# A gather put ahead of two loads, a shorter sort and a first product in parts, at the start of a fused expert kernel

## What is computed

```python
def xattn(h, token_ids, ctx):              # 4 experts, chosen by token id
    e = min(clip(token_ids, 0, 24999) // 6250, 3)
    return (silu(h @ ctx[e].T) * (h @ ctx[e].T)) @ ctx[e].T

def ffn(h, router_w, wg, wu, wd):          # 8 experts, chosen by argmax of the router
    e = argmax(h @ router_w.T)
    g, u = bitlinear(h, wg[e]), bitlinear(h, wu[e])
    return bitlinear(square(relu(g)) * u, wd[e])

x = x + xattn(layernorm(x), token_ids, ctx)
x = x + ffn(layernorm(x), router_w, wg, wu, wd)
```

## Time and profile before

| | us |
|---|---|
| three runs | 279.82, 280.27, 280.93; median 280.27 |
| the profiled execution | 279.12 |
| its span, first to last instruction | 277.3 |
| TensorE busy | 243.5 (88%) |
| VectorE busy | 221.8 (80%) |
| ScalarE busy | 213.1 (77%) |
| GpSimd busy | 154.9 (56%) |

### The profile page before, as it was taken

The page is one execution under the profiler, slowest core; times in us unless marked ns, Lnnn a source line. Parts: engine busy times, 40 slices in busy tenths (PEclk is TensorE's granted clock), DMA queues, the critical chain, the costliest instruction groups (busy, mean ns, idle before and its releaser), DMA issues.

```text
span 277.3 us, 5763 instructions
## 1 busy us (share of the span) xinstructions
PE 243.5 (88%) x1419; PEld 175.5 (63%) x1419; DVE 221.8 (80%) x664; ACT 213.1 (77%) x322; POOL 154.9 (56%) x277
## 2 busy tenths in 40 slices
PE   2287779999999999999999999886699999999980
PEld 2134558888888888888888888762344555545440
DVE  5958797889877887778878877898968888888871
ACT  2778778798887998879889788855468888888860
POOL 3435013576565655656656553487547487576743
PEclk9997999999999999999999999999779999999996
DMA  5999259356646664956656534440486994201110
GB/s 214 430 372 345 60 195 384 109 214 224 219 156 227 208 194 154 329 183 232 227 190 219 162 131 175 146 128 8 107 294 191 306 278 173 78 34 66 57 41 0
DMA packets 13839, 51.72 MB, mean 186 GB/s; under 512 B 2862, under 2 KB 2862, under 8 KB 10224
## 3 DMA queue, kind: packets, MB, share of 16 engines
q1 hardware_dynamic: 8928, 37.91, 39.9%
q0 software_dynamic: 4880, 13.44, 13.8%
HBM read 40.49 MB, written 13.48 MB: 195 GB/s over the span
## 4 chain that ended last, share of the span: by engine, by line
PE 74%; DVE 12%; issue 6%; ACT 3%; POOL 2%; DMA 1%; DVEq 0%; POOLq 0%
PE bank L1294 36%; PE bank L1397 19%; PE bank L1287 9%; PE bank L1369 5%; PE bank L1391 4%; PE bank L1313 1%; POOL x L412 1%; DVE ctx_lo L791 1%; POOL out_rows L505 1%; DVE fac L1113 1%; DVE ternary L759 1%; DVE prod L1103 1%; ACT relu L632 1%; ACT ternary L542 1%; DMA token_ids<-token_ids_in 1%
## 5 line engine op out<-in xcount | busy, mean ns | idle before, releaser
L1397 PE MATMUL bank<-ternary,qT 128*128 x184 | 45.0, 388 | 0.4 <-ACT qT L620 0.3
L542 ACT ACTIVATE ternary<-staged 128x2048 bf16<-128x2048 f32 x22 | 42.0, 1910 | 1.3 <-DMA staged<-weight_chunks 1.2
L548 ACT ACTIVATE ternary<-staged,w_scale 128x1536 int16<-128x1536 f32 x22 | 34.4, 1566 | 2.8 <-DVE w_scale L803 2.8
L1397 PEld LDWEIGHTS bank<-ternary,qT 128*128 128x128 bf16 x184 | 18.2, 100 | 22.3 <-issue 4.7
L451 POOL DMA_INDIRECT x_rows<-row,store_at x19 | 22.2, 1168 | 16.7 <-POOL store_at L447 14.4
L412 POOL DMA_INDIRECT x<-x_rows,gather x19 | 21.1, 1108 | 18.7 <-DVE row L897 14.8
L1397 PE MATMUL bank<-ternary,rT 128*128 x92 | 24.6, 392 | 2.6 <-DVE late_rows L1132 1.2
L505 POOL DMA_INDIRECT out_rows<-late_rows x18 | 19.1, 1060 | 13.3 <-DVE late_rows L1132 10.4
L422 POOL TENSOR_TENSOR rstd<-var_eps,half_powers 128x1 f32<-128x1 f32 x19 | 13.6, 714 | 21.6 <-DVE var_eps L855 21.2
L1294 PE MATMUL bank<-ctx_hi,hT_hi 128*128 x76 | 23.3, 429 | 0.6 <-DVE hT_lo L871 0.5
L576 ACT ACTIVATE pT_hi<-bank 128x512 fp32r<-128x512 f32 x19 | 11.4, 597 | 15.9 <-PE bank L1287 15.9
(11 more groups left out here) (213 smaller groups left out, 656.6 us busy)
## 6 DMA issues: line engine op xcount, KB each, us to landing
staged<-weight_chunks SPq DMA_DIRECT2D x22, 1024.0 KB, 5.2
late_rows<-x_rows SPq DMA_DIRECT2D x18, 260.0 KB, 3.4
ternary<-ctx_chunks SPq DMA_DIRECT2D x4, 1024.0 KB, 10.9
x_rows<-filler SPq DMA_DIRECT2D x9, 260.0 KB, 2.8
ternary<-weight_chunks SPq DMA_DIRECT2D x2, 1024.0 KB, 6.4
staged<-x_rows SPq DMA_DIRECT2D x5, 260.0 KB, 3.1
x<-x_rows,gather POOLq DMA_INDIRECT x19, 3.6
x_rows<-row,store_at POOLq DMA_INDIRECT x19, 3.3
```

The lines of the kernel that those rows point to most:

```text
L542: nc.scalar.activation(ternary[:, m * K * D:(m + 1) * K * D], staged[i % 2][:, :], ACT.Abs, accum_out=abs_sum[:, 2 * i:2 * i + 1]).then_in ...
L548: nc.scalar.activation(ternary[:, m * K * D + DVE_COLS:(m + 1) * K * D].bitcast(I16), staged[i % 2][:, DVE_COLS:], ACT.Copy, scale=w_scale ...
L1397: last = pe.matmul(ps[:, :], left[:, k * P:(k + 1) * P], ternary[:, bass.ds(e * (3 * K * D) + (kind * K + k) * D, D)], start=(k == 0), sto ...
```

## The change

**Queue of SyncE.** The loads of contexts 2 and 3 wait until the first gather has been issued. **Sort.** Rounding is left to the conversion to int32 when a result is written; the count matmul has 1/128 in place of ones, in a tile that GpSimd fills once the integer iota has been read; the token number is multiplied in at `row_hot` rather than at `block_hot`; the expert numbers are made after the gather's indices. **First product.** It starts once the high half of h and of context 0 are there, and waits for the low halves inside; the low halves of a context are made in two instructions. **Order.** ScalarE, VectorE and TensorE take the pieces of the first blocks in a new order, and the second `warm_up` has 3 matmuls for 8. The later products wait for constants, not for their expert's number.

```diff
@@ -59,7 +56,7 @@
 
 RING, ROWS = 4, 3
 
-WARM_UP = (4, 8, 4)
+WARM_UP = (4, 3, 4)
 
 
 TICKS, STEPS = B1 + 1, B2 + 5
...
@@ -326,6 +326,8 @@
             load_weights(0)
             load_context(1)
             load_weights(1)
+
+            sp.wait_ge(gathering, 1)
             load_context(2)
             load_context(3)
             for i in range(2, len(ORDER)):
...
@@ -399,10 +401,13 @@
             for r in row:
                 pool.memset(r[:, TOKEN + 1:], 0.0).then_inc(made, 1)
 
+            pool.wait_ge(iota_read, 1)
+            pool.memset(part_of_block, 1.0 / P).then_inc(part_made, 1)
+
             pool.wait_ge(placing, 1)
             for t in range(POOL_TILES):
-                pool.tensor_scalar(row_hot[:, t, :], iota16[:, :], place_row[:, t:t + 1], None, ALU.is_equal)\
-                    .then_inc(pool_hot_ready, 1)
+                pool.tensor_scalar(row_hot[:, t, :], iota16[:, :], place_row[:, t:t + 1], token1[:, t:t + 1],
+                                   ALU.is_equal, ALU.mult).then_inc(pool_hot_ready, 1)
 
             def gather(b):
                 if not 0 <= b < B1:
...
@@ -653,18 +658,18 @@
             high_halves(1)
             sum_abs(1)
             scale_part(0)
+            evict_hT(0)
+            scale_part(1)
             high_halves(2)
-            scale_part(1)
-            evict_hT(0)
-            high_halves(3)
-            sum_abs(2)
             silu(0)
             evict_hT(1)
+            sum_abs(2)
             evict_pT(0)
+            high_halves(3)
             scale_part(2)
-            sum_abs(3)
             silu(1)
             evict_hT(2)
+            sum_abs(3)
             scale_part(3)
             sum_abs(4)
             for t in range(2, TICKS):
...
@@ -735,46 +741,45 @@
             dve.tensor_scalar(ebase[:, :], iota[:, 0:E2], float(CAP), None, ALU.mult)
 
             dve.wait_ge(sort_pe, 1)
-            link(dve.tensor_scalar(blocks, count_ps, 1.0 / P, 0.5 - 0.5 / P, ALU.mult, ALU.add))
-            link(dve.tensor_scalar(blocks, blocks, MAGIC, MAGIC, ALU.add, ALU.subtract))
-            link(dve.scalar_tensor_tensor(excess, blocks, float(P), count_ps, ALU.mult, ALU.subtract))
+
+            link(dve.tensor_scalar(blocks, count_ps, 1.0 / P, 0.5 - 0.5 / P, ALU.max, ALU.add))
+            link(dve.tensor_tensor(excess, blocks, count_ps, ALU.subtract))
             link(dve.tensor_tensor_scan(excess_sum, ones[:, 0:E1], excess, 0.0, ALU.mult, ALU.add))
             link(dve.tensor_tensor(lift, excess_sum, excess, ALU.subtract))
             wide = [P, E1, TILES]
             rank3 = bank[7][:, 0:E1 * TILES].rearrange("p (e t) -> p e t", e=E1)
             placed3 = placed[:, :].rearrange("p (e t) -> p e t", e=E1)
-            link(dve.tensor_tensor(placed3, rank3, small[:, 5, :, None].to_broadcast(wide), ALU.add))
+            link(dve.scalar_tensor_tensor(placed3, small[:, 5, :, None].to_broadcast(wide), float(P), rank3,
+                                          ALU.mult, ALU.add))
             link(dve.tensor_tensor(placed3, placed3, m3, ALU.mult))
             link(dve.tensor_reduce(place[:, :], placed[:, :].rearrange("p (e t) -> p t e", e=E1), X, ALU.add))
             link(dve.tensor_scalar(place_block[:, :], place[:, :], 1.0 / P, 0.5 / P - 0.5, ALU.mult, ALU.add))
-            link(dve.tensor_scalar(place_block[:, :], place_block[:, :], MAGIC, MAGIC, ALU.add, ALU.subtract))
             dve.scalar_tensor_tensor(place_row[:, :], place_block[:, :], -float(P), place[:, :], ALU.mult, ALU.add)\
                 .then_inc(placing, 1)
             wide = [P, TILES, B1]
-            link(dve.tensor_tensor(block_hot, iota[:, None, 0:B1].to_broadcast(wide),
-                                   place_block[:, :, None].to_broadcast(wide), ALU.is_equal))
-            dve.tensor_tensor(block_hot, block_hot, token1[:, :, None].to_broadcast(wide), ALU.mult)
+            dve.tensor_tensor(block_hot, iota[:, None, 0:B1].to_broadcast(wide),
+                              place_block[:, :, None].to_broadcast(wide), ALU.is_equal)
             dve.wait_ge(placing, 1)
             for t in range(POOL_TILES, TILES):
-                dve.tensor_scalar(row_hot[:, t, :], iota16[:, :], place_row[:, t:t + 1], None, ALU.is_equal)\
-                    .then_inc(hot_ready, 1)
+                dve.tensor_scalar(row_hot[:, t, :], iota16[:, :], place_row[:, t:t + 1], token1[:, t:t + 1],
+                                  ALU.is_equal, ALU.mult).then_inc(hot_ready, 1)
 
             link(dve.tensor_tensor_scan(blocks_sum, ones[:, 0:E1], blocks, 0.0, ALU.mult, ALU.add))
             link(dve.tensor_tensor(start, blocks_sum, blocks, ALU.subtract))
+
+
+            table_ps = bank[6][:, 0:B1]
+            dve.wait_ge(sort_pe, 2)
+            link(dve.tensor_scalar(pad1[:, :], table_ps, 0.0, None, ALU.is_equal))
+            dve.scalar_tensor_tensor(gather1[:, :], table_ps, -1.0, pad1[:, :], ALU.add, ALU.add).then_inc(sorted1, 1)
             wide = [P, B1, E1 - 1]
             started13 = started1[:, :].rearrange("p (b e) -> p b e", b=B1)
             link(dve.tensor_tensor(started13, iota[:, 0:B1, None].to_broadcast(wide),
                                    small[:, 4:5, 1:].to_broadcast(wide), ALU.is_ge))
             link(dve.tensor_reduce(expert1_f[:, :], started13, X, ALU.add))
             dve.tensor_copy(expert1[:, :], expert1_f[:, :]).then_inc(experts1_ready, 1)
-
-
-            table_ps = bank[6][:, 0:B1]
-            dve.wait_ge(sort_pe, 2)
-            link(dve.tensor_scalar(pad1[:, :], table_ps, 0.0, None, ALU.is_equal))
-            link(dve.scalar_tensor_tensor(gather1[:, :], table_ps, -1.0, pad1[:, :], ALU.add, ALU.add))
-            dve.sem_inc(sorted1, 1)
             dve.tensor_scalar(valid[:, :], table_ps, 0.0, None, ALU.is_gt).then_inc(table_read, 1)
+            dve.wait_ge(sorted1, 1)
             dve.tensor_scalar(pad1[:, :], pad1[:, :], BEYOND, None, ALU.mult).then_inc(tables1_ready, 1)
             dve.tensor_copy(ones16[:, :], ones[:, :])
             dve.tensor_scalar(from16[:, :], before[:, :], -1.0, 1.0, ALU.mult, ALU.add)
...
@@ -1264,7 +1278,8 @@
             width = E1 * TILES
             pe.matmul(bank[7][:, 0:width], before[:, :], member[:, :], start=True, stop=False)
             pe.matmul(bank[7][:, 0:width], ones[:, :], earlier[:, :], start=False, stop=True)
-            pe.matmul(bank[7][:, 256:256 + E1], ones[:, :], small[:, 6, :], start=True,
+            pe.wait_ge(part_made, 1)
+            pe.matmul(bank[7][:, 256:256 + E1], part_of_block, small[:, 6, :], start=True,
                       stop=True).then_inc(sort_pe, 1)
             pe.wait_ge(router_sum_ready, 1)
             pe.matmul(router_ps, ones[:, :], router_sum[:, :], start=True, stop=True).then_inc(router_mean_ready, 1)
...
@@ -1287,9 +1302,13 @@
                     last = pe.transpose(ps[:, k * P:(k + 1) * P], src[:, k * P:(k + 1) * P], ident[:, :])
                 return last
 
-            def product1(ps, hi, lo, e):
+            def product1(ps, hi, lo, e, first=False):
                 pairs = [(hi, ctx_hi), (hi, ctx_lo), (lo, ctx_hi)]
                 for n, (left, right) in enumerate(pairs):
+                    if first and n == 1:
+                        pe.wait_ge(ctx_lo_ready, 1)
+                    if first and n == 2:
+                        pe.wait_ge(hT_lo_ready, 1)
                     for k in range(K):
                         last = pe.matmul(ps[:, :], left[:, k * P:(k + 1) * P],
                                          right[:, bass.ds(e * (K * D) + k * D, D)],
...
@@ -1324,16 +1343,18 @@
             def first_product(b):
                 if not 0 <= b < B1:
                     return
-                pe.wait_ge(hT_lo_ready, b + 1)
+                if b == 0:
+
+                    pe.wait_ge(hT_hi_ready, 1)
+                    pe.wait_ge(ctx_hi_ready, 1)
+                    pe.wait_ge(centred, 1)
+                else:
+                    pe.wait_ge(hT_lo_ready, b + 1)
                 if b >= 2:
                     pe.wait_ge(p_ready, b - 1)
-                if b == 0:
-                    pe.wait_ge(centred, 1)
-                if b < 5:
-                    pe.wait_ge(ctx_lo_ready, expert_of[b] + 1)
-                elif b == 5:
-                    pe.wait_ge(ctx_lo_ready, E1)
-                product1(a_ps[b % 2], hT_hi, hT_lo, expert_of[b]).then_inc(a_ready, 1)
+                if 1 <= b < E1:
+                    pe.wait_ge(ctx_lo_ready, b + 1)
+                product1(a_ps[b % 2], hT_hi, hT_lo, expert_of[b], b == 0).then_inc(a_ready, 1)
 
             def transpose_p(b):
                 if not 0 <= b < B1:
...
@@ -1474,9 +1495,9 @@
                     pe.matmul(bank[3][:, :], iota16[:, :], iota16[:, None, :].to_broadcast([P, K, P]),
                               start=True, stop=True)
 
+            sum_mean(0)
             pe.wait_ge(experts1_ready, 1)
             load_expert(0)
-            sum_mean(0)
             warm_up(WARM_UP[0])
```

(10 more changed lines are left out.)

50 lines of the change are left out of this document (29 added, 21 removed).

## The result

| | us |
|---|---|
| before, median of 4 runs | 280.04 |
| after, median of 4 runs | 284.84 (283.85 to 284.93) |
| ratio after to before | 1.0172, 95% interval 1.0133 to 1.0212 |
| profiled execution after, its span | 284.93, 283.1 |

The change makes the kernel slower by 1.7%, where I forecast no change (280.0, range up to 281.5). The span grew by 5.8 us, from 277.3 to 283.1.

A forecast was written before the change was run, and what follows sets the result against it. The start of block 2's first product, behind a weight sum on ScalarE, was taken as the gate: 25.9 + 14.8 = 40.7 for 40.97, 0.3 us earlier, hence 280.0 us, range 277.9 to 281.5.

The forecast's parts named there:

- What bounds the kernel: Start of block 2's first product at 40.97 us gates the steady part, released by ScalarE's sum of matrix 4.
- The sort: Sort edits ahead of the first gather: the gather goes out at 13.2, 0.6 us earlier.
- The gather: First gather ahead of contexts 2 and 3: lands 3.6 us after issue, at 16.8 for 19.77, 3.0 us earlier.
- To the first product: From the gather's landing to the first product: it starts at 22.6 for 24.43, 1.8 us earlier.
- a: End of the first product, just ahead of silu's start: forecast 25.9 for 28.53, 2.7 us earlier.
- n: Number of the first product's matmuls at the lower clock, 0.22 us more each: taken as 1, ends 0 and 12.
- From a to the restart: From the first product's end to block 2's product: 14.8 us for 12.4, costing 2.4 of the 2.7 us won.
- That product 3.04: Block 1's first product on TensorE, started at a + 3.85: taken to last 3.04 us.
- the walk: Queue-by-queue reckoning after a: block 1's product starts at a + 3.85, the restart comes at a + 14.8.
- Behind it TensorE is full, so this passes to the end: After block 2's product starts: the 0.3 us gained there passes whole to the end, execution 278.8.
- The slower rival: Whole first product at 1.2 GHz, as seven warm-ups do not raise the clock: a = 28.3, 282.4 us; chance 0.06.
- the sum's 40.7: Forecast start of block 2's product: 25.9 + 14.8 = 40.7 for 40.97, 0.3 us earlier.

The follow-up runs named there:

- product_first: Changed kernel with 3 and 5 unread matmuls around the transposes of p(0), and block 2's product ahead of the sum of matrix 4 on TensorE: 281.30 us, ratio 1.0046.
- sort_only: Kernel before with the sort's edits alone: 279.57 us, ratio 0.9991.
- combined: Changed kernel with matrix 0's mean first, eight warm-ups, three GpSimd rows, first gap filled, block 2's product ahead of matrix 4's sum, six fillers behind: 279.05 us, ratio 0.9974.
- fill_first: Changed kernel with unread matmuls only around the transposes of p(0), 3 ahead and 5 behind: 282.91 us, ratio 1.0100.
- fill_both: Changed kernel with unread matmuls, 3 ahead of and 5 behind the transposes of p(0), 11 ahead of the sum of matrix 4: 280.29 us, ratio 1.0024.
- jump_only: Kernel before with one edit, SyncE waiting for the first gather ahead of contexts 2 and 3: 282.03 us, ratio 1.0108.
- no_jump: Changed kernel without SyncE's wait for the gather ahead of contexts 2 and 3: 287.35 us, ratio 1.0250.
- combined_full: The combined kernel with 8 more unread matmuls in the waits it still had: 278.85 us over 12 runs, ratio 0.9959.

## Why the prediction was wrong

**What bounds the kernel: right in the main.** The restart of block 2's product waits for the sum of matrix 4; product_first shows it by moving that product to 37.99. But it was not the only gate into the steady part: moving it gained 1.6 us and not 3, as waits for VectorE stand behind it.

**The sort: wrong in size.** I took 0.1 us for GpSimd's second scalar, with twice the length as the other end; it measured 0.2 a row (3.62 for 2.76 in four), and TensorE's table waits for the last of them. VectorE's was 0.05, as taken. The gather left at 13.89, not 13.2, and sort_only shows no gain at all. With one row less on GpSimd (combined) the indices come at 11.63.

**The gather: right.** 3.7 us to land, taken 3.6. No wait of ScalarE for contexts 2 and 3. But the loads put behind it did cost where I had written nothing: I said of matrix 2 only that its own wait is later. I did not follow what its load then meets, the two contexts still in flight. It took 7.37 us, where the loads of matrices 2 and 3 had taken 5.2 and 5.4 before, and held its sum by 0.8.

**To the first product: right, partly by luck.** 22.38 for 22.6, transposes queued behind the sum of matrix 1 and the warm-ups, a at 25.47 for 25.9. Two misses mostly cancel: the transposes started 0.5 late (20.54 for 20.05), and the last warm-ups took 1.0 us up to the product where I had 1.5. The product ran at full clock, n = 0 rather than 1; in fill_first and product_first, whose TensorE does the same up to there, its first four matmuls took 1.70 and 2.20 us, about n = 2 and 4.

**From a to the restart: this step failed.** "The restart comes at a + 14.8": it came at a + 18.3. The term that was mis-sized is "That product 3.04". It measured 5.34, 2.3 of the 3.5 us; the other 1.2 are its start, a + 5.06 instead of 3.85. Most of that is VectorE: I let the gate of block 0 follow silu at once, but the first half subtraction of context 1 stands ahead of it in the queue and ended at 27.01, so the gate started at a + 1.45 for 0.62 and the second half ended at 29.94. The rest is the sum of matrix 2, which came last. With the clock kept and 0.57 of the load's wait gone, fill_both measured a + 15.5 (41.32 from 25.83), its product starting at a + 4.5 behind that second half: 0.7 more than the walk.

**"Behind it TensorE is full, so this passes to the end": failed too.** Block 2's product was given the length of one at full clock, and took 2.4 us more, with the granted clock at 0.50. I had priced a matmul at the lower clock (0.22 us each, twelve are 2.64) and applied it to the first product only. My own walk held the warning: it has TensorE ending the transposes of p(0) near a + 2.1 and starting the product at a + 3.85, and ending the transposes of p(1) at a + 11 with nothing to do until a + 14.5. Before, the clock had fallen once in the start, near 23.4, 1.2 us after TensorE came back from an idle piece of 1.9 us, 20.3 to 22.2:

```profile
23.25:23.50 0.25, 0.25 (x3) 0.00 (x0) 0.25 (x2) 0.25 (x2) 0.25 (x1) 0.64 1.04 408
```

It had not fallen behind another piece of 1.92. So pieces of 1.8 and 3.5 us were two such risks, and I named none.

**The slower rival** had the right mechanism at the wrong place, the first product, and for the wrong cause, the missing warm-ups. The page of the Trainium skill that I cited ("TensorE: Matmul & The Clock Gate", Part 1) says the other half as well: a long idle wait throttles again, and the next burst starts slow. The trace agrees in the direction: granted clock 0.50 behind the pieces that begin at 28.3 and 39.8 us, and fill_both takes it away. In the length it does not: the waits that the page has in mind are longer than the first of these pieces (1.76 us), and jump_only kept its clock over one of 3.54.

With the clock kept the sum comes near: fill_both is 0.5 us above the kernel before of its session (279.75), where the sum has 0.3 below. That is inside the range; most of the 0.8 between is the restart, 41.32 for the sum's 40.7.

## What to carry to other kernels

When an edit moves work from ahead of a point to behind it, walk TensorE's queue on both sides and write down each idle piece. Where the trace already shows a fall of the clock near an idle piece of that size, price the burst behind it at the slow length too, as a rival with a fair chance. It is a chance and no certainty: here the clock fell near pieces of 1.76, 1.90 and 1.94 us and stayed up over others of 1.92 and 3.54. A wait that is put into a load queue gains or loses by what the consumers ask for first: here the same line was worth 2.5 us in one order and nothing, or a loss, in the other. And where a kernel's start has such pieces that cannot be closed, matmuls that nobody reads, into a free bank, are the cheap remedy (4.1 to 4.6 us here), to be tried before the order is blamed.

## What the runs showed of the hardware

A second per-partition scalar and a second operation on a 128 x 128 f16 row cost GpSimd 0.2 us (0.69 to 0.91) and VectorE 0.05 (0.18 to 0.23).

How fast the first product starts differs from one execution to the next more than with the number of warm-ups. Its first four matmuls took 1.25, 1.27, 1.70 and 2.20 us in the profiled executions of after, fill_both, fill_first and product_first, where TensorE does the same up to there (seven matmuls ahead of the transposes, four behind). With twelve ahead they took 2.07 in the kernel before and 1.20 in sort_only.

The granted clock reads 1.00 in the first 20 us of the profiles before and after, though warm-ups of 512 columns took 0.42 us each there, and 0.23 later in the same kernels (fill_both, 11 in 2.54 us at 37.30). So in this stretch the spacing tells the speed and the column does not. The row of the kernel before for one us of its eight warm-ups in 3.35 us:

```profile
17.00:18.00 1.00, 1.00 (x4) 0.32 (x3) 1.00 (x2) 1.00 (x2) 0.00 (x0) 1.00 1.05 442
```

The small gather landed 6.0 us after its issue with contexts 2 and 3 in flight, 6.6 in no_jump, and after 3.7 and 3.8 with them held back (after, jump_only). The second gather of the changed kernel, issued at 15.4 beside them, took 7.9.

The same kernel spreads by several us: 276.7 to 281.8 for combined_full in twelve runs, 278.0 to 283.1 for the kernel before in the 26 of the same session, 283.85 to 284.93 for the changed kernel in only four. What decides it is open.
